# Pairwise field projection on one core: x loaded two tiles at a time into four buffers, the first four tiles' x ahead of all stores

## The reference

```python
# x: (2048, 32, 64) float32, W: (496, 64, 64) float32
PAIRS = np.array(list(combinations(range(32), 2)))   # 496 pairs i < j
xi = x[:, PAIRS[:, 0], :]
xj = x[:, PAIRS[:, 1], :]
proj = jnp.einsum('bpd,pod->bpo', xi, W)
return proj * xj                                      # (2048, 496, 64) float32
```

## Time and profile before

| | |
|---|---|
| median of 3 runs | 692.61 us (691.69 to 692.86) |
| the profiled execution | 691.5 us |
| its span, first to last instruction | 689.7 us |
| mean granted TensorE clock | 0.904 |
| moved by DMA | 285.16 MB, 413 GB/s over the span |
| busy: PE, DVE, ACT, POOL | 595.4, 415.0, 205.1, 390.7 us |

### The profile page before, as it was taken

One profiled execution on the slowest core, in us unless ns is written; L12 is line 12 of the kernel. 1 busy time (PEld: TensorE's weight loads), 2 busy tenths in 40 slices (PEclk: granted clock), 3 DMA queues, 4 the chain that ended last, 5 costly groups with the idle time before them and its releaser, 6 DMA issues.

```text
span 689.7 us, 8297 instructions
## 1 busy us (share of the span) xinstructions
PE 595.4 (86%) x2704; PEld 370.3 (54%) x2704; DVE 415.0 (60%) x528; ACT 205.1 (30%) x257; POOL 390.7 (57%) x228
## 2 busy tenths in 40 slices
PE   6969979799797979979799797979979799797972
PEld 4636646465464646646466464645646466464541
DVE  1657647486574756646576574756647576474851
ACT  2412414233241422414233241422414224141320
POOL 0735737556473745738557474755728557374651
PEclk9988989899898997989989898998979989898995
DMA  8999999999999999999999999999999999999897
GB/s 341 398 427 425 430 428 426 426 422 428 420 427 427 419 426 394 425 421 416 428 402 429 409 430 426 412 424 411 425 425 378 422 409 424 414 431 425 362 419 310
DMA packets 29755, 285.16 MB, mean 413 GB/s; under 512 B 3312, under 2 KB 3440, under 8 KB 7216
## 3 DMA queue, kind: packets, MB, share of 16 engines
q1 hardware_dynamic: 29600, 284.96, 99.1%
q10 hardware_dynamic: 144, 0.07, 0.0%
HBM read 24.97 MB, written 260.05 MB: 413 GB/s over the span
## 4 chain that ended last, share of the span: by engine, by line
DMA 37%; POOL 26%; issue 22%; PE 10%; ACT 2%; DVE 1%; POOLq 0%; SPq 0%; DVEq 0%; ACTq 0%
DMA out_dram<-staged 36%; POOL staged L228 26%; PE proj L288 9%; ACT staged L254 2%; DVE staged L330 1%; DMA ident_sb<-ident_dram 1%; PE proj L305 1%; POOLq L227 0%; PE proj L266 0%; ACT x_t L243 0%; SPq L182 0%; POOLq L120 0%; ACTq L253 0%; DVEq L125 0%; SPq L181 0%
## 5 line engine op out<-in xcount | busy, mean ns | idle before, releaser
L288 PE MATMUL proj<-w_sb,x_t 64*128 64x512 f32 (+7 forms) x2432 | 561.8, 563 | 75.6 <-DVE staged L330 73.2
L330 DVE TENSOR_TENSOR staged<-proj,x_sb 128x1024 f32<-128x1024 f32 (+7 forms) x528 | 415.0, 828 | 263.8 <-PE proj L288 183.0
L228 POOL TENSOR_TENSOR staged<-staged,x_sb 128x1024 f32<-128x1024 f32 (+4 forms) x224 | 390.5, 1755 | 283.9 <-ACT staged L254 283.2
L288 PEld LDWEIGHTS proj<-w_sb,x_t 64*128 64x128 f32 x2432 | 338.4, 205 | 291.8 <-issue 134.1
L254 ACT ACTIVATE staged<-proj 128x1024 f32<-128x1024 f32 (+4 forms) x224 | 172.8, 787 | 455.5 <-PE proj L288 344.0
L243 ACT ACTIVATE x_t<-proj 128x1024 f32<-128x1024 f32 x32 | 31.0, 1021 | 10.6 <-PE proj L266 9.1
L266 PEld LDWEIGHTS proj<-ident_sb,x_sb 128*128 128x128 f32 x256 | 28.6, 143 | 8.8 <-issue 7.6
L266 PE MATMUL proj<-ident_sb,x_sb 128*128 128x128 f32 x256 | 32.2, 280 | 0.6 <-DMA x_sb<-x_dram 0.6
L305 PE MATMUL proj<-ident_sb 128*128 128x128 f32 x16 | 3.7, 421 | 5.5 <-DMA ident_sb<-ident_dram 5.5
L305 PEld LDWEIGHTS proj<-ident_sb 128*128 128x128 f32 x16 | 3.3, 223 | 5.5 <-DMA ident_sb<-ident_dram 5.5
L243 ACT ACT_TABLE_LOAD x1 | 1.3, 1283 | 1.2 <-PEq L360 1.2
## 6 DMA issues: line engine op xcount, KB each, us to landing
out_dram<-staged SPq DMA_DIRECT2D x16, 1952.0 KB, 11.4
out_dram<-staged SPq DMA_DIRECT2D x16, 1824.0 KB, 14.1
out_dram<-staged SPq DMA_DIRECT2D x16, 1728.0 KB, 17.3
out_dram<-staged SPq DMA_DIRECT2D x16, 1696.0 KB, 14.7
out_dram<-staged SPq DMA_DIRECT2D x16, 1568.0 KB, 14.3
out_dram<-staged SPq DMA_DIRECT2D x16, 1440.0 KB, 15.6
out_dram<-staged SPq DMA_DIRECT2D x16, 1312.0 KB, 15.6
out_dram<-staged SPq DMA_DIRECT2D x16, 1216.0 KB, 12.1
```

What stands on the lines that cost most here:

```text
L228: last = nc.gpsimd.tensor_tensor(product, product, x_sb[tile.parity][:, j * dim:(j + n) * dim], ALU.mult)
L288: last = nc.tensor.matmul(proj[b][h][:, at:at + width], x_t[tile.parity][half, i // 2, :], w_sb[half, col:col + width], start=True, stop=True)
L330: last = nc.vector.tensor_tensor(staged_part(item, i, j, n), proj[b][h][:, at:at + n * dim], x_sb[tile.parity][:, j * dim:(j + n) * dim], ...
```

## The change

There are four buffers for x in place of two. x of the tiles 0 to 3 is loaded before any store is issued. After that x is loaded for two tiles at once, after the stores of every second tile: x of tiles 4 and 5 after tile 1, of 6 and 7 after tile 3, and so on to 14 and 15 after tile 11. To make room in SBUF, the area that is reserved for descriptors of DMAs is set to 1 KB of each partition, in place of 16 KB. The loops of all engines, SP's too, now have four tiles in a body and three turns, with one tile written out ahead and three behind. Each reader of x takes the buffer by the tile's place in four, and each buffer has its own semaphore.

```diff
+DMA_SCRATCH = 1024
...
-    def __init__(self, number, parity, half, last=False):
-        self.number, self.parity, self.half, self.last = number, parity, half, last
-        self.first = isinstance(number, int) and number == 0
+    def __init__(self, turn, quarter, last=False):
+        self.number, self.turn, self.quarter, self.last = 4 * turn + quarter, turn, quarter, last
+        self.parity = quarter % 2
+        self.first = isinstance(turn, int) and turn == quarter == 0
...
     def each_tile(eng, emit):
-        emit(Tile(0, 0, 0))
-        with eng.Fori(0, (tiles - 2) // 2) as t:
-            emit(Tile(2 * t + 1, 1, t))
-            emit(Tile(2 * t + 2, 0, t + 1))
-        emit(Tile(tiles - 1, 1, tiles // 2 - 1, last=True))
+        emit(Tile(0, 0))
+        with eng.Fori(0, tiles // 4 - 1) as t:
+            for quarter in range(1, 4):
+                emit(Tile(t, quarter))
+            emit(Tile(t + 1, 0))
+        for quarter in range(1, 4):
+            emit(Tile(tiles // 4 - 1, quarter, last=quarter == 3))
...
-        x_sb = [sb(f"x_sb{h}", [P, fields * dim]) for h in range(2)]
+        x_sb = [sb(f"x_sb{q}", [P, fields * dim]) for q in range(4)]
...
-            def load_x(tile):
-
-                sp.dma_start(x_sb[tile.parity][:], x[bass.ds((tile.number + 2) * P, P), :]
-                             ).then_inc(x_loaded[tile.parity], 16)
+            def load_x(turn, quarter):
+                sp.dma_start(x_sb[quarter][:], x[bass.ds((4 * turn + quarter) * P, P), :]
+                             ).then_inc(x_loaded[quarter], 16)
+
+            def emit_and_load(tile):
+                emit(tile)
+                if tile.quarter == 1 and not isinstance(tile.turn, int):
+                    load_x(tile.turn + 1, 0)
+                    load_x(tile.turn + 1, 1)
+                elif tile.quarter == 3 and not tile.last:
+                    load_x(tile.turn + 1, 2)
+                    load_x(tile.turn + 1, 3)
...
-            sp.dma_start(x_sb[1][:], x[P:2 * P, :]).then_inc(x_loaded[1], 16)
-
-            tile = Tile(0, 0, 0)
-            emit(tile)
-            load_x(tile)
-            with sp.Fori(0, (tiles - 4) // 2) as t:
-                for tile in (Tile(2 * t + 1, 1, t), Tile(2 * t + 2, 0, t + 1)):
-                    emit(tile)
-                    load_x(tile)
-            tile = Tile(tiles - 3, 1, tiles // 2 - 2)
-            emit(tile)
-            load_x(tile)
-            emit(Tile(tiles - 2, 0, tiles // 2 - 1))
-            emit(Tile(tiles - 1, 1, tiles // 2 - 1, last=True))
+            for quarter in range(1, 4):
+                load_x(0, quarter)
+            each_tile(sp, emit_and_load)
...
-                        pe.wait_ge(x_loaded[1 - tile.parity], 16 * tile.half + 16)
+                        pe.wait_ge(x_loaded[(tile.quarter + 1) % 4], 16 * tile.turn + 16)
                         for h in range(2):
                             pe.wait_ge(emptied[b][h], use)
-                            turn(b, 1 - tile.parity, h)
+                            turn(b, (tile.quarter + 1) % 4, h)
...
-    nc = bacc.Bacc("TRN2", target_bir_lowering=False, num_devices=1)
+    nc = bacc.Bacc("TRN2", target_bir_lowering=False, num_devices=1,
+                   dynamic_dma_scratch_size=DMA_SCRATCH)
```

More of the change, by code:

```diff
@@ L75, in field_pair_project @@
     w_at, w_ends = w_columns(fields, dim)
-    assert 2 * dim == P and fields == 32 and tiles % 2 == 0 and tiles >= 4
+    assert 2 * dim == P and fields == 32 and tiles % 4 == 0 and tiles >= 8
     assert all(2 * c == fields * dim for c in (UNIT,))
@@ L144, in field_pair_project @@
         x_first_loaded = [sem(f"x_first_loaded{h}") for h in range(2)]
-        x_loaded = [sem(f"x_loaded{h}") for h in range(2)]
+        x_loaded = [sem(f"x_loaded{q}") for q in range(4)]
         w_loaded = [sem(f"w_loaded{c}") for c in range(len(w_cuts) - 1)]
@@ L228, in emit @@
                         last = nc.gpsimd.tensor_tensor(
-                            product, product, x_sb[tile.parity][:, j * dim:(j + n) * dim], ALU.mult)
+                            product, product, x_sb[tile.quarter][:, j * dim:(j + n) * dim], ALU.mult)
                     g = group_of[item]
@@ L331, in emit @@
                                 staged_part(item, i, j, n), proj[b][h][:, at:at + n * dim],
-                                x_sb[tile.parity][:, j * dim:(j + n) * dim], ALU.mult)
+                                x_sb[tile.quarter][:, j * dim:(j + n) * dim], ALU.mult)
                         last.then_inc(emptied[b][h], 1)
```

## The result

The changed kernel takes **699.01 us** (median of 4 runs, 698.31 to 699.48), against 692.15 for the kernel before, measured beside it: ratio 1.0103, 95% interval 1.0091 to 1.0115. It is slower, and by more than the range of the prediction allowed. The profiled execution took 698.31 us with a span of 696.5, 6.8 more than the span before.

A forecast was written before the change was run, and what follows sets the result against it. Bytes through one DMA queue, paced by its last engine, were taken to set the time. All terms were 0 except +0.5 for code, on 692.61: 693.1 us, range 689.6 to 697.6.

The forecast's parts named there:

- Twelve other loads in six pairs: x loads after tiles 1, 3, 5, 7, 9 and 11: same bytes, steps alternate 38.9 and 43.9 us, cost 0.
- Changeovers between stores and reads: DMA queue: eight fewer switches between stores and x loads, worth nothing to 3.0 us gained; taken as 0.
- Loads ahead: Tiles 2 and 3 loaded before the stores: first resumption moves from 51.39 to 56.4 us, later minus 5.0, sum 0.
- Steps without x: Steps between ACT's resumptions with no x load: 38.9 us each, no loss from the slowest DMA engine running dry.
- Rival B: The 0.46 us excess belongs to each step without x: eight new ones, +3.7, 696.3 us; chance 0.14.
- rival C: Last DMA engine runs dry after a pair, as longer stalls delay group 0's store: +6, 698.6 us; chance 0.08.
- rival D: PE's four-tile loop body isn't held and is fetched again each turn: +3 to +11, say 698 us; chance 0.10.
- Cover of the slow engine: Before group 0's store flows, the last DMA engine keeps 2.1 to 3.0 us of older work in steps newly without x.
- Code: Instruction queues: about 11 more packets for longer programs, 0 to 5 us on the last DMA engine, taken as +0.5.
- The four-tile body: PE's loop body grows from 672 to 1344 matmul and weight-load instructions; the two-tile body is held, refetching kept as a rival.
- Rival E: Descriptor area has to do with the slow DMA engine: minus 0.8 in 15 steps, 681 us; chance 0.02.
- Changeovers (A): Rival: switches between stores and reads cost the last DMA engine 0.38 us each: minus 3.0, 689.6 us; chance 0.15.

The follow-up runs named there:

- fillers: Changed kernel plus 1 MB of extra DMA in the steps without x: as a store 712.68 us (1.0301), as a load 712.34 us (1.0292).
- step 4: Kernel before, group 0's store held back until DVE's half of the plan's fourth step is emptied: 692.28 us, ratio 1.0005.
- step 5: Kernel before, group 0's store held back until DVE's half of the plan's fifth step is emptied: 696.07 us, ratio 1.0061.

## Why the prediction was wrong

The step that failed is "Twelve other loads in six pairs [...] the same bytes", cost 0, together with "Changeovers between stores and reads", whose lower bound was nothing and whose upper was a gain of 3.0 us. It excluded that fewer and larger reads could be dearer. In fact the six long steps took 45.0 us on average in place of 43.9: 6.4 us, nearly all of the 6.9 by which the kernel is slower.

The reasoning error behind it: in the step as a whole I found an x load worth 2.05 to 2.5 us and took that as a price of the load. It is the price of a load **in a row of steps that all have one**. Fourteen loads of the trace before had one in the step just before (or the loads at the start), so no row there shows a load after a step without one. That was the unmeasured quantity, and I bounded it on one side only. Rows showed the direction: the dip to 263 GB/s at full share was known, and I priced it only as something to save.

The other steps:
- **Loads ahead**, sum 0: the first resumption came at 56.63, forecast 56.4. The first load that follows also follows a step without one, so the loads ahead have a price after all: with one load per step afterwards, this load costs the slow engine 4.0 us for 2.5. That is 1.5 of the 2.1 us by which that kernel is slower than the one before; the two instruction packets in the step of 42.07 may be most of the rest.
- **Steps without x**: 38.99 on average against 38.92. Rival B, which gave the 0.46 to the step, is refuted as a cause. Its time, 696.3, was nearer than the forecast's, and those of C, 698.6, and D, 698, nearer still; all three mechanisms are refuted, so their nearness is luck.
- **Cover of the slow engine**: it held. In the two stretches between stores that I cut by microseconds (143 to 175 and 228 to 244 us) the lowest share is 0.36. Group 0 landed no less than 8.1 us after its issue in any tile, where rival C asked for less than 6.5. C is refuted.
- **Code**: 9 more packets (11 forecast). What they cost no row isolates. The end took 18.94 us for 18.42, but no instruction packet falls in it, and the step ahead of it is shorter by as much (38.91 for 39.38). The +0.5 is neither confirmed nor refuted.
- **The four-tile body**: between 226 and 587 us the kernel after has no instruction packet at all, so the longer body is held too and rival D is refuted. The rule of the Trainium skill, "Runtime: NRT & Kernel Launch", section on instruction fetch mechanics, that a branch beyond a two-page window forces a fetch, is not borne out by the trace at either length. The prediction left out that the same section gives PE room for 2048 instructions, more than the 1344 matmuls and weight loads of the longer body; with that figure the trace agrees. The queue view of that stretch has one row:

```profile
q1 hardware_dynamic: 14752, 148.11, 99.1%
```

- **Area**, 0: measured 1.0005. Rival E is refuted.
- **Changeovers (A)**, a gain: fewer of them gave no gain to be seen. The long steps are dearer, not cheaper.

**What is shown, and what isn't.** Shown: the loss sits in the steps with loads, and with one load in every step 5.3 of the 6.9 us are gone. It does not need the pair, its size, its adjacency, a long gap without reads, the area or the long body: a single load after a step without one is dear too. A step without a load isn't needed either: with fillers, pairs are dear in four of six cases. Shown too: a slow stretch at full share costs a step nothing when the slow engine's own load doesn't fall into it, as in the kernel with the load in mid-tile. Where the others were slow, the single loads part cleanly by how far behind that engine was: free at 4.1 us and more, dear at 3.9 and less.

My best reading: when an x load comes up, the fifteen engines sometimes read together and slowly for some microseconds. A slow engine that is far enough behind reads after them, at full speed; one that has caught up reads with them and shares the slow time. A step without a load lets it catch up, and a pair lasts so long that even an engine 5 to 6 us behind is caught by the second load. This is argued, not shown: no run changed that engine's lag alone and made a slow stretch dear by it. The held-back store changed it, but its four dear loads had no slow stretch beside them, and they stay outside this reading. Open too is why the others are slow at some loads and not at others; a long time without a load isn't needed for it, nor a step without one, since the mid-tile loads had neither ahead of them.

## What to carry to other kernels

Where a kernel runs at the bytes of its queue, spread the loads evenly among the stores: bunching the same bytes into every second step cost 1%, though not one byte, wait or instruction count spoke against it. When a trace shows an event in one rhythm only, its price holds for that rhythm; for another, put a bound on both sides of zero. And read GB/s beside the DMA share: a dip with a low share is an idle engine and may be free; a dip at full share is slow work, and it costs only if the engine that sets the pace is in it.

## What the runs showed of the hardware

- One load of 1 MB among stores brought sixteen busy DMA engines to 241 to 350 GB/s for 5 us (the kernel with half the loads), where they otherwise move 426.
- The same load cost the slowest engine 2.5 us in a steady rhythm, 4.0 us after a step without a load, and 3.55 in a dear step of the kernel with the held-back store.
- One of the sixteen DMA engines is slower than the others on this queue: in the kernel before it completes each DMA of 300 to 640 us 3.8 to 6.4 us after the other fifteen. Three splits of x suggest the third to fifth engine, if rows are dealt out in order.
- A slow stretch of the other fifteen (344 to 359 GB/s over 9 us, at a share of 0.99 to 1.00) was free while the slow engine was 4.5 to 5.6 us behind.
- Holding group 0's store back was free up to step 4. At step 5 it made four of the steps 1.2 us longer, those in which the slow engine was 1.5 to 2.1 us behind the first.
